# Second half of layer 0: a ring of seven gather buffers instead of four, and gathers issued six tiles ahead instead of four

## The chip, the cores and the metric

The kernel runs on one core of a Trainium2 chip. A core has five engines with a queue of instructions each: TensorE (PE, with its weight loads PEld), VectorE (DVE), ScalarE (ACT), GpSimd (POOL) and SyncE (SP). They run side by side and are tied together only by semaphores that one engine raises and another waits for. Data moves between main memory and the core's buffers by DMA, which an engine issues and which then runs by itself. The metric is the device time of one execution in microseconds (us); here the median of three runs.

## The reference, cut to what matters

The model is four graph layers over 10,000 nodes with 512 features and 10,000 edges. Layer 0 is

```python
def gnn_layer(x, W, b, src, dst):
    h = x @ W.T + b
    msgs = h[src]
    agg = jax.ops.segment_sum(msgs, dst, num_segments=N_NODES)
    return jax.nn.relu(agg)

h = gnn_layer(x, W1, b1, src, dst)
out = gnn_layer(h, W2, b2, src, dst)
...
h = jnp.maximum(_layernorm(x, axis=-1), 0.0)
x = x + _L0_gnn_ref(h, edge_index, L0_gnn_W1, L0_gnn_b1, L0_gnn_W2, L0_gnn_b2)
```

The change touches the second `gnn_layer` call (W2, b2), with the sum onto x and the layer norm's scale and bias that follow it. Rows of h are picked by source node, rows with the same destination are summed, the sums are multiplied with W2, and the result goes back to the row of its node.

## The kernel before, in words

The edges have been sorted by destination beforehand and cut into 79 tiles of 128 edges (`ET`). `layer0(..., second=True)` is the stretch from about 686 to 1058 us of the profiled execution; its buffers and semaphores carry the prefix `b_`. The sum is taken before the product, since both are linear. Per tile, all written out (no loop on the chip):

- POOL issues three indirect DMAs. `start_fetch` (L1054, the DMA in `fetch`, L815) gathers 128 rows of h into a buffer `b_G`; `residual` (also L815) gathers the rows of x that are added later into `b_xr`; `store` (`put_rows`, L819) scatters the finished rows `b_rows`. Every eighth tile POOL also computes the scales and biases of the layer norm for eight tiles (L886, L893).
- PE, in `sum_edges` (L1356), multiplies the gathered rows with a 0/1 matrix `b_sel`, which sums rows of one destination, into `b_pt` (raises `s_summed`); in `multiply` (L794 to L796) it multiplies the sums, split in a high and a low part, with W2 into `b_po` (raises `s_prod`); in `look` (L1404) it does a small look-up product for a later layer.
- DVE waits for `s_summed`, carries an open sum over from the tile before (L784, L787), takes relu(product)+x into `b_rows` (L1220, raises `s_rows`), makes the low part (L1204), the row statistics and the look-up's result (L857, L866, L1293).
- ACT waits for DVE's carry, makes the high part (L1120), six small operations that build 0/1 matrices, and last presets the product's accumulator with the bias (L1164, `b_po<-b_brow`), without which PE's next product doesn't start.

PE's order is: sum of tile u+1, product of tile u, look-up of tile u. DVE's order at step u is: carry of tile u+1, `b_rows` of tile u-1, low part of tile u+1, statistics of tile u-1. The order of POOL is given by `at(i, u, offset, ...)` in its `body`: at step u it issues the gather of tile u+4, the gather of x for tile u+2 and the store of tile u-10, in that order, so the first store comes at step 10. POOL's instructions run strictly in this order, and each wait holds up everything behind it.

Two waits on POOL matter here. The gather of tile T may overwrite its buffer only when the tile that used it four tiles ago has been summed: `wait(pool, s_summed, T.t - 3)`. With T = u+4 that is the sum of tile u. The gather of x for tile T = u+2 waits for `b_rows` of tile u-2 (`wait(pool, s_rows, T.t - 3)`).

Of the kernel before, what the change touches and what calls it, by code (L numbers as in the profile page):

```python
# [19 lines left out]
P = 128  # L20
D = 512
C = D // P
EXT = 520
# [7 lines left out]
F32, F32R, BF16 = mybir.dt.float32, mybir.dt.float32r, mybir.dt.bfloat16  # L31
# [25 lines left out]
def at(i, u, off, unroll, tiles, stage):  # L57

    tile = Tile(i + (u + off) // unroll, (u + off) % unroll, unroll)
    if not isinstance(i, int) or 0 <= tile.t < tiles:  # L60
        stage(tile)
# [17 lines left out]
def wait(eng, sem, value):  # L79

    if not isinstance(value, int) or value > 0:
        eng.wait_ge(sem, value)
# [886 lines left out]
def layer0(nc, io, g, second):  # L969
# [4 lines left out]
    NT, N, ET = g.NT, g.N, g.tiles  # L974
    U = 4
    GR = -(-ET // U)

    QUAD, RING = 8, 16 if second else 4
    LATE = 2
    if not second:  # L980
        g.hold2 = ExitStack()
        g.qrow16 = g.hold2.enter_context(nc.sbuf_tensor("qrow16", [NT, N], I16))
    qrow16 = g.qrow16
    with ExitStack() as ctx:
        e = Env(nc, ctx, "b_" if second else "a_")
# [2 lines left out]
        if second:  # L988
            s_preset = e.sem("s_preset")
        neg_half = e.sb("neghalf", [P, QUAD], F32)  # L990
        G = e.ring("G", U, [P, D if second else EXT], F32)
        sel = e.ring("sel", 2, [P, P], F32)
        carry = e.ring("carry", 2, [P, C], F32)
        Thi, Tlo = e.ring("Thi", 2, [P, C, P], F32R), e.ring("Tlo", 2, [P, C, P], F32R)
# [28 lines left out]

        s_brow, s_const = e.sem("s_brow"), e.sem("s_const")
        s_Gn = e.sem("s_Gn")
        s_G, s_x, s_put = e.sems("s_G", U), e.sems("s_x", U), e.sems("s_put", RING)
        s_sel = e.sem("s_sel")
        s_summed, s_carried, s_copied = e.sem("s_summed"), e.sem("s_carried"), e.sem("s_copied")
        s_Thi, s_Tlo = e.sem("s_Thi"), e.sem("s_Tlo")
# [21 lines left out]
        @block.gpsimd  # L1051
        def _(pool):
            def start_fetch(T):
                s = T.slot(U)  # L1054
                wait(pool, s_summed, T.t - 3)
                fetch(pool, G[s][:, :], src, index(g, "D", T, 0)).then_inc(s_G[s], 16)

            def residual(T):
                s = T.slot(U)
                wait(pool, s_rows, T.t - 3)  # L1060
                fetch(pool, xr[s][:, :], io.x, index(g, "D", T, 1)).then_inc(s_x[s], 16)

            def scales(T):
                n = ln.part(T)[1] if ln.in_last(T) else QUAD
                some = slice(T.slot(RING), T.slot(RING) + n)
                ln.make_scales(pool, T, neg_half, rows[:, some, SCALE])
                ln.make_biases(pool, T, rows[:, some, SCALE], rows[:, some, BIAS])

            def store(T):
                s = T.slot(RING)  # L1070
                if second:
                    pool.wait_ge(ln.s_bias, ln.done(T))
                else:
                    pool.wait_ge(s_rows, T.t + 1)
                put_rows(pool, g.xs[0] if second else g.h1, index(g, "D", T, 2), rows[:, s, :], N - 1)\
                    .then_inc(s_put[s], 16)

            def body(i):
                if second:
                    for u in range(RING):  # L1080
                        if u % QUAD == LATE:
                            at(i, u, -QUAD - LATE, RING, EARLY, scales)
                        at(i, u, 4, RING, ET, start_fetch)
                        at(i, u, 2, RING, ET, residual)
                        at(i, u, -QUAD - LATE, RING, EARLY, store)
                else:
                    for u in range(U):
                        at(i, u, -2, U, ET, store)
                        at(i, u, 4, U, ET, start_fetch)

            if second:
                pool.memset(one_f[:, :], 1.0)
            pool.memset(neg_half[:, :], -0.5).then_inc(s_const, 1)
            for s in range(2):
                pool.memset(carry[s][:, :], 0.0).then_inc(s_const, 1)
            if second:
                pool.memset(rows[:, :, BIAS + 1:EXT], 0.0).then_inc(s_const, 1)
            pool.wait_ge(s_const, 4 if second else 3)
            straight(-(-ET // RING), 1, 1, body, between=W and (lambda i: W.low_part(pool, i)))
            if second:  # L1100
                for first, n in LAST:
                    scales(Tile(0, first, ET))
                    for t in range(first, first + n):
                        store(Tile(0, t, ET))
            for s in range(RING):
                pool.wait_ge(s_put[s], 16 * uses(ET, RING, s))
# [239 lines left out]
        def _(pe):  # L1346
            def sum_edges(T):
                s = T.slot(2)
                pe.wait_ge(s_sel, T.t + 1)
                if second:  # L1350
                    pe.wait_ge(s_G[T.slot(U)], 16 * (T.use(U) + 1))
                else:
                    pe.wait_ge(s_Gn, T.t + 1)
                wait(pe, s_Tlo, T.t - 1)
                for c in range(C):
                    ins = pe.matmul(psum_t[s][:, c, :], G[T.slot(U)][:, c * P:(c + 1) * P], sel[s][:, :],  # L1356
                                    start=True, stop=True)
                ins.then_inc(s_summed, 1)

# [910 lines left out]
```

## Time and profile before

| | us |
|---|---|
| median of 3 runs (2797.72 to 2799.21) | 2798.69 |
| the profiled execution's own time | 2799.54 |
| its span in the profile | 2797.8 |
| PE busy in the span | 2459.9 (88%) |
| DVE, ACT, POOL busy | 2024.5 (72%), 1373.6 (49%), 1709.9 (61%) |

The profiled execution lies 0.85 us above the median; 1.7 us of it lie outside the span. Times in the rows further down are microseconds from the span's start. A row of the timeline gives start, duration, engine, line of the kernel, operation, output<-input and how many were merged; in brackets stands how long the engine was idle before it and what ended that. Matmuls are pipelined, and their ends are modelled. For a DMA that POOL issues, the row is the issue alone; the transfer itself comes later.

### The profile page before, as it was taken

Reading aid. Unit: us, or ns where it says so; the run is one execution under the profiler, and the core shown is the slowest. Engines: PE = TensorE matmul, PEld = TensorE weight load, DVE = VectorE, ACT = ScalarE, POOL = GpSimd, SP = SyncE. Lnnn points to the kernel's source line nnn. Section 1 sums busy time; section 2 is a strip of 40 time slices with the busy share of each in tenths; the row PEclk is TensorE's granted clock in tenths of the full one; section 3 lists DMA queues with packets and bytes.
Section 4 is the critical chain, followed back from the end, with each engine's and each line's share of the span. In section 5 each row is a group of like instructions: output and inputs, shape, how many; then the busy total and the mean of one; then the engine's idle time right before and its main releaser. Section 6 shows DMA issues by size and latency. Waiting matters only on the chain. (4 is left out here: it accounts for less than half of the span.)

```text
span 2797.8 us, 46999 instructions
## 1 busy us (share of the span) xinstructions
PE 2459.9 (88%) x13660; PEld 2095.8 (75%) x13660; DVE 2024.5 (72%) x5281; ACT 1373.6 (49%) x2875; POOL 1709.9 (61%) x1832
## 2 busy tenths in 40 slices
PE   3555379998988886999999969999999699999998
PEld 3344268887877776999999958888888588888886
DVE  7777666664655554888877869999999666666666
ACT  1555334454776764555555523333333245555553
POOL 0565345554566765777777647777777445555553
PEclk9999999999999998999999989999999799999999
DMA  8677643533444543343333333333334245555553
GB/s 246 206 209 206 196 125 113 146 119 114 127 134 145 156 151 127 111 129 115 113 118 114 107 110 123 114 115 114 116 120 121 85 139 153 153 153 153 153 152 110
DMA packets 145287, 385.55 MB, mean 138 GB/s; under 512 B 34127, under 2 KB 34287, under 8 KB 144554
## 3 DMA queue, kind: packets, MB, share of 16 engines
q0 software_dynamic: 100144, 300.93, 36.0%
q1 hardware_dynamic: 45002, 83.04, 9.5%
q8 instruction: 52, 0.85, 0.1%
q14 instruction: 89, 0.73, 0.1%
HBM read 259.61 MB, written 148.26 MB: 146 GB/s over the span
## 5 line engine op out<-in xcount | busy, mean ns | idle before, releaser
L1830 ACT CAST d_Thi<-d_pt 128x512 fp32r<-128x512 f32 x79 | 46.4, 587 | 307.8 <-DVE d_pt L787 276.7
L1678 PE MATMUL c_pu<-c_Zhi,parts 128*128 128x256 f32 x640 | 182.0, 284 | 5.3 <-DVE c_Zlo L1596 5.3
L1680 PE MATMUL c_pu<-c_Zhi,parts 128*128 128x256 f32 x640 | 181.8, 284 | 0.0
L1679 PE MATMUL c_pu<-c_Zlo,parts 128*128 128x256 f32 x640 | 180.6, 282 | 0.0
L815 POOL DMA_INDIRECT f_Gsrc<-rows,indexS x79 | 76.0, 962 | 170.4 <-PE f_phsrc L2159 161.4
L2075 ACT ACTIVATE f_Mhi<-f_pm 128x512 fp32r<-128x512 f32 x79 | 47.3, 598 | 262.2 <-DVE f_pm L2108 255.6
L2099 DVE TENSOR_TENSOR f_Hlosrc<-f_phsrc,f_Hhisrc 128x512 fp32r<-128x512 f32 x79 | 54.6, 692 | 159.6 <-ACT f_Hhisrc L2069 127.7
L794 PE MATMUL b_po<-parts,b_Thi 128*128 128x512 f32 x316 | 132.4, 419 | 41.0 <-issue 26.1
L819 POOL DMA_INDIRECT h<-a_rows,indexD x79 | 79.6, 1008 | 117.7 <-ACT a_rows L1172 109.0
L1565 ACT ACTIVATE c_pu<-c_pu,c_b1col 128x256 f32<-128x256 f32 x160 | 61.6, 448 | 167.6 <-PE c_pu L1680 167.6
L794 PE MATMUL d_po<-parts,d_Hhi 128*128 128x512 f32 x316 | 131.2, 415 | 1.9 <-DVE d_Hlo L1848 1.9
L794 PE MATMUL a_po<-parts,a_Thi 128*128 128x512 f32 x316 | 130.7, 414 | 0.5 <-DVE a_Tlo L1204 0.4
L794 PE MATMUL c_po<-parts,c_Uhi 128*128 128x512 f32 x316 | 127.8, 404 | 0.0
L1678 PEld LDWEIGHTS c_pu<-c_Zhi,parts 128*128 128x128 f32 x640 | 121.4, 190 | 7.6 <-DVE c_Zlo L1596 5.8
L795 PE MATMUL b_po<-parts,b_Thi 128*128 128x512 f32 x316 | 126.0, 399 | 0.0
L794 PE MATMUL f_pm<-parts,f_Hhidst 128*128 128x512 f32 x316 | 125.9, 399 | 0.0
L796 PE MATMUL f_pm<-parts,f_Hlosrc 128*128 128x512 f32 x316 | 125.9, 398 | 0.0
L796 PE MATMUL b_po<-parts,b_Tlo 128*128 128x512 f32 x316 | 125.7, 398 | 0.0
L434 POOL DMA_INDIRECT edgesD<-r_cargoD,r_posiD x79 | 75.7, 958 | 81.7 <-DVE r_posiS L399 33.2
L795 PE MATMUL f_pm<-parts,f_Hhisrc 128*128 128x512 f32 x316 | 125.5, 397 | 0.0
L795 PE MATMUL f_pm<-parts,f_Hhidst 128*128 128x512 f32 x316 | 125.2, 396 | 0.0
L794 PE MATMUL f_pm<-parts,f_Hhisrc 128*128 128x512 f32 x316 | 125.1, 396 | 0.0
(451 smaller groups left out, 9548.0 us busy)
## 6 DMA issues: line engine op xcount, KB each, us to landing
rows<-r_xt SPq DMA_DIRECT2D x40, 520.0 KB
h<-q_zerorow SPq DMA_DIRECT2D x80, 256.0 KB
r_xt<-in_x SPq DMA_DIRECT2D x80, 256.0 KB
a_wstage<-in_L_W SPq DMA_DIRECT2D x3, 1024.0 KB
selrowsD<-selD SPq DMA_DIRECT2D x1, 2640.0 KB
selrowsS<-selS SPq DMA_DIRECT2D x1, 2640.0 KB
q_keyrowD<-in_dst POOLq DMA_DIRECT2D x1, 2560.0 KB, 17.0
q_keyrowS<-in_src POOLq DMA_DIRECT2D x1, 2560.0 KB
```

What stands on the lines that cost most here:

```text
L434: pool.indirect_dma_start(g.sorted[k], bass.IndirectOffsetOnAxis(ap=posi[k][r][:, 0:1], axis=0), cargo[k][r][:, :], None).then_inc(q_moved ...
L794: ins = pe.matmul(out, hi[:, c, :], whi[:, c, :], start=start and c == 0, stop=False, skip_group_check=preset)
L795: ins = pe.matmul(out, hi[:, c, :], wlo[:, c, :], start=False, stop=False, skip_group_check=preset)
L796: ins = pe.matmul(out, lo[:, c, :], whi[:, c, :], start=False, stop=stop and c == C - 1, skip_group_check=preset)
L815: return pool.indirect_dma_start(out, None, table, bass.IndirectOffsetOnAxis(ap=rows, axis=0))
L819: return pool.indirect_dma_start(table, bass.IndirectOffsetOnAxis(ap=at_rows, axis=0), rows, None, bounds_check=last_row, oob_is_err=False)
L1565: ins = nc.scalar.activation(psum_u[:, c, :], psum_u[:, c, :], ACT.Relu, bias=b1col[:, c:c + 1])
L1678: pe.matmul(psum_u[:, o, :], g.Whi[2][:, c, cols], Zhi[:, c, :], start=c == 0, stop=False)
L1679: pe.matmul(psum_u[:, o, :], g.Whi[2][:, c, cols], Zlo[:, c, :], start=False, stop=False)
L1680: ins = pe.matmul(psum_u[:, o, :], g.Wlo[2][:, c, cols], Zhi[:, c, :], start=False, stop=c == C - 1)
L2075: nc.scalar.activation(Mhi[s][:, :], psum_m[s][:, :], ACT.Relu).then_inc(s_Mhi, 1)
L2099: dve.tensor_tensor(Hlo[k][s][:, :, :], psum_h[k][:, :, :], Hhi[k][s][:, :, :].bitcast(F32), ALU.subtract).then_inc(s_Hlo[k], 1)
```

## The change

In the second half the ring of gather buffers and their semaphores grows from 4 to 7 (`AHEAD`), the gather at step u is the one of tile u+6 instead of u+4, and it waits until the tile seven before it has been summed: with T = u+6 that is the sum of tile u-1 instead of tile u. PE reads the tile from the longer ring. The ring of x (`xr`), the stores, and the first half of the layer stay as they were.

```diff
+    AHEAD = 7 if second else 4
...
-        G = e.ring("G", U, [P, D if second else EXT], F32)
+        G = e.ring("G", AHEAD, [P, D if second else EXT], F32)
...
-        s_G, s_x, s_put = e.sems("s_G", U), e.sems("s_x", U), e.sems("s_put", RING)
+        s_G, s_x, s_put = e.sems("s_G", AHEAD), e.sems("s_x", U), e.sems("s_put", RING)
...
             def start_fetch(T):
-                s = T.slot(U)
-                wait(pool, s_summed, T.t - 3)
+                s = T.slot(AHEAD)
+                wait(pool, s_summed, T.t - AHEAD + 1)
                 fetch(pool, G[s][:, :], src, index(g, "D", T, 0)).then_inc(s_G[s], 16)
...
-                        at(i, u, 4, RING, ET, start_fetch)
+                        at(i, u, 6, RING, ET, start_fetch)
                         at(i, u, 2, RING, ET, residual)
                         at(i, u, -QUAD - LATE, RING, EARLY, store)
...
                 if second:
-                    pe.wait_ge(s_G[T.slot(U)], 16 * (T.use(U) + 1))
+                    pe.wait_ge(s_G[T.slot(AHEAD)], 16 * (T.use(AHEAD) + 1))
...
-                    ins = pe.matmul(psum_t[s][:, c, :], G[T.slot(U)][:, c * P:(c + 1) * P], sel[s][:, :],
+                    ins = pe.matmul(psum_t[s][:, c, :], G[T.slot(AHEAD)][:, c * P:(c + 1) * P], sel[s][:, :],
```

POOL's instructions at the start of the half, before the change (`b_G` gathers of h, `b_xr` gathers of x):

```order
L1097 MEMSET b_rows 128x16x6
L815 DMA b_G<-h,indexD 128x512 x3
L815 DMA b_xr<-in_x,indexD 128x512
L815 DMA b_G<-h,indexD 128x512
L815 DMA b_xr<-in_x,indexD 128x512
```

The same place with the change:

```order
L1098 MEMSET b_rows 128x16x6
L815 DMA b_G<-h,indexD 128x512 x5
L815 DMA b_xr<-in_x,indexD 128x512
L815 DMA b_G<-h,indexD 128x512
L815 DMA b_xr<-in_x,indexD 128x512
```

Two more gathers of h stand ahead of the first gather of x. From there on the two kinds alternate as before, each `b_G` now for a tile two further on. At the end of the half, POOL's instructions of before and of the change differ as follows (stores are `rows<-b_rows`):

```order
 L815 DMA b_xr<-in_x,indexD 128x512
 L819 DMA rows<-b_rows,indexD 10241x520
-L815 DMA b_G<-h,indexD 128x512
 L815 DMA b_xr<-in_x,indexD 128x512
 L819 DMA rows<-b_rows,indexD 10241x520
 L886 TENSOR_TENSOR b_rows<-b_lnvar,b_neghalf 128x8
 L893 TENSOR_TENSOR b_rows<-b_lnminus,b_rows 128x8
-L815 DMA b_G<-h,indexD 128x512
 L815 DMA b_xr<-in_x,indexD 128x512
 L819 DMA rows<-b_rows,indexD 10241x520
```

The last two gathers have moved up by two steps and are gone here. On PE, DVE and ACT the instructions and their order stay the same.

## Rows read from the trace of the kernel before

**Rows 1.** Windows: per engine busy us (count), then PE's granted clock, DMA share, GB/s.
```profile
700.00:740.00 40.00, 39.98 (x219) 33.74 (x218) 26.91 (x82) 31.82 (x79) 21.84 (x23) 1.00 0.43 123
740.00:1020.00 280.00, 246.17 (x1347) 208.12 (x1347) 163.24 (x499) 195.61 (x487) 192.47 (x198) 1.00 0.48 145
```

**Rows 2.** Waits, 686 to 1060 us: us in total, times, longest.
```profile
DVE b_carry L784 <- PE b_pt L1356: 121.0, 44, 11.3
...
POOL b_G L815 <- PE b_pt L1356: 53.2, 31, 2.6
...
PE b_pt L1356 <- DMA b_G<-h,indexD: 9.9, 1, 9.9
```

**Rows 3.** Timeline of PE before the first store: the sums of two tiles.
```profile
707.75 1.06 PE L1356 MATMUL b_pt<-b_sel,b_G 128*128 128x128 f32 x8
...
715.82 1.06 PE L1356 MATMUL b_pt<-b_sel,b_G 128*128 128x128 f32 x8
```

**Rows 4.** Timeline of DVE before the first store: the carry behind the first of them.
```profile
708.84 0.22 DVE L784 SCALAR_TENSOR_TENSOR b_carry<-b_carry,keylastD,b_pt 128x4 f32<-128x4 f32 x1 [1.28 <-PE b_pt L1356]
```

**Rows 5.** Timeline of PE in mid-half: a sum, and the next product's start.
```profile
850.41 1.06 PE L1356 MATMUL b_pt<-b_sel,b_G 128*128 128x128 f32 x8
...
856.74 0.47 PE L794 MATMUL b_po<-parts,b_Thi 128*128 128x512 f32 x1 [1.36 <-issue]
```

**Rows 6.** Timeline of DVE: a late carry, the `b_rows` behind it, the next late carry.
```profile
852.86 0.22 DVE L784 SCALAR_TENSOR_TENSOR b_carry<-b_carry,keylastD,b_pt 128x4 f32<-128x4 f32 x1 [3.28 <-PE b_pt L1356]
...
853.12 0.68 DVE L1220 SCALAR_TENSOR_TENSOR b_rows<-b_po,b_xr 128x512 f32<-128x512 f32 x1
...
862.00 0.22 DVE L784 SCALAR_TENSOR_TENSOR b_carry<-b_carry,keylastD,b_pt 128x4 f32<-128x4 f32 x1 [2.99 <-PE b_pt L1356]
```

**Rows 7.** Timeline of ACT: the preset that this product waits for.
```profile
855.92 0.67 ACT L1164 ACTIVATE b_po<-b_brow,degcol 128x512 f32<-128x512 f32 x1
```

**Rows 8.** Timeline of POOL in mid-half: issues of one double step.
```profile
853.10 0.97 POOL L815 DMA_INDIRECT b_G<-h,indexD  x1 [1.54 <-PE b_pt L1356]
854.38 0.95 POOL L815 DMA_INDIRECT b_xr<-in_x,indexD  x1 [0.30 <-issue]
855.62 1.01 POOL L819 DMA_INDIRECT rows<-b_rows,indexD  x1 [0.30 <-issue]
856.94 0.97 POOL L815 DMA_INDIRECT b_G<-h,indexD  x1 [0.30 <-issue]
858.22 0.95 POOL L815 DMA_INDIRECT b_xr<-in_x,indexD  x1 [0.30 <-issue]
859.47 1.01 POOL L819 DMA_INDIRECT rows<-b_rows,indexD  x1 [0.30 <-issue]
```

**Rows 9.** Timeline of DVE: first and last of the late carries, 32 double steps apart.
```profile
742.82 0.22 DVE L784 SCALAR_TENSOR_TENSOR b_carry<-b_carry,keylastD,b_pt 128x4 f32<-128x4 f32 x1 [2.95 <-DMA r_xt<-in_x]
...
1035.16 0.22 DVE L784 SCALAR_TENSOR_TENSOR b_carry<-b_carry,keylastD,b_pt 128x4 f32<-128x4 f32 x1 [1.97 <-PE b_pt L1356]
```

**Rows 10.** Timeline of POOL after its last gather of h: a wait for `b_rows`.
```profile
1032.93 1.02 POOL L819 DMA_INDIRECT rows<-b_rows,indexD  x1 [0.30 <-issue]
1036.38 0.98 POOL L815 DMA_INDIRECT b_xr<-in_x,indexD  x1 [2.43 <-DVE b_rows L1220]
```

**Rows 11.** Timeline of POOL in the layer's first half: a store, then a gather.
```profile
594.04 1.01 POOL L819 DMA_INDIRECT h<-a_rows,indexD  x1 [0.37 <-issue]
...
595.36 0.97 POOL L815 DMA_INDIRECT a_G<-rows,indexD  x1 [0.30 <-issue]
```

**Rows 12.** Timeline of PE and DVE there: the sum, and the carry behind it.
```profile
595.21 1.06 PE L1356 MATMUL a_pt<-a_sel,a_G 128*128 128x128 f32 x8
...
597.31 0.22 DVE L784 SCALAR_TENSOR_TENSOR a_carry<-a_carry,keylastD,a_pt 128x4 f32<-128x4 f32 x1 [1.26 <-PE a_pt L1356]
```

**Rows 13.** Timeline, first half, another place: POOL's gather and DVE's carry.
```profile
567.86 0.97 POOL L815 DMA_INDIRECT a_G<-rows,indexD  x1 [0.30 <-issue]
...
569.59 0.22 DVE L784 SCALAR_TENSOR_TENSOR a_carry<-a_carry,keylastD,a_pt 128x4 f32<-128x4 f32 x1
```

## The prediction, on record before the changed kernel ran

> **What bounds the kernel now.** I read the windows first, then the waits, then the timeline of each engine. Layer 0's second half has two regimes. Before the first store PE is busy 39.98 of 40 us; afterwards 246.17 of 280 us, at a granted clock of 1.00 in both, so about 34 us of PE's time are lost in the second regime [rows 1]. Among the waits DVE's for PE's sum is the largest (121.0 us); POOL waits 53.2 us for the same sum; PE waits for a gathered tile once in the whole half, 9.9 us at its start [rows 2]. So no gather is late after the first, and fetching earlier cannot help PE by that road.
>
> The timelines say what the second regime waits for. Early, two tiles take 715.82-707.75 = 8.07 us on PE [rows 3], and DVE's carry starts 0.03 us after the modelled end of the sum (707.75+1.06 = 708.81 against 708.84) [rows 3, 4]. In mid-half a sum ends by the model at 850.41+1.06 = 851.47, and DVE's carry, idle for 3.28 us, starts only at 852.86, 1.39 us later [rows 5, 6]; POOL, which waits for the same sum, goes on at 853.10 [rows 8]. Two engines wake together, so it is PE's signal that comes late, not DVE. From the carry on the chain is tight: ACT's preset runs 855.92 to 856.59 [rows 7], and PE's product, idle for 1.36 us, starts at 856.74 [rows 5]. Every second tile is like this: late carries stand 862.00-852.86 = 9.14 us apart [rows 6], and over 32 double steps (1035.16-742.82)/32 = 9.14 us [rows 9], against 8.07.
>
> What makes the signal late? POOL issues six transfers in a row, 0.30 us apart, then stops to wait for the sum. Its last issue before the stop is the store at 859.47, and the late carry comes at 862.00, 2.53 us behind it [rows 6, 8]. At the end of the half, where the row of issues ends with the store at 1032.93, the carry comes at 1035.16, 2.23 us behind it [rows 9, 10]. I read this as a loop: PE's signals get through about 2.2 to 2.5 us after POOL's last issue of a dense row, and POOL starts its next row only on that signal. The trace shows no cause inside the chip; the lag is what I use. One turn is carry to gather 853.10-852.86 = 0.24, gather to last store 859.47-853.10 = 6.37, store to carry 2.53; sum 9.14 [rows 6, 8].
>
> **The change, part by part.** *Seven buffers.* PE, DVE and ACT execute the same instructions; another buffer number costs nothing. *Earlier start.* Two gathers of h move ahead of the first gather of x, which is issued 2 x 1.28 us later [rows 8]. It is needed first behind the first product, and DVE's b_rows comes behind the carry anyway: I take 0; if that cover were absent, 2.6 us. The first regime stays at 8.07 us for two tiles, since POOL there has two transfers per tile only.
>
> *The moved wait.* At step u the gather now needs the sum of tile u-1, which is long done when POOL gets there. POOL doesn't stop there any more, but one instruction later, at the gather of x, which waits for b_rows of tile u-2. DVE makes those rows behind the late carry: carry 852.86, b_rows 853.12+0.68 = 853.80 [rows 6]. Queued behind this wait are the store, the next gather and the rest of the row. So the row of six is now x, store, gather, x, store, gather, and it ends with a gather. Its turn of the loop:
> - carry to x: the one place that shows it has the carry at 1035.16 and the x gather, released by b_rows, at 1036.38: 1.22 us [rows 9, 10] (instead of 0.24).
> - x to last gather: x to store 1.24, to gather 1.32, to x 1.28, to store 1.25, to gather 1.32 as the one before: 6.41 us [rows 8] (instead of 6.37).
> - last gather to carry: not shown in this half, where every such row ends with a store. In the layer's first half a store at 594.04 is followed by a gather at 595.36; the sum ends by the model at 595.21+1.06 = 596.27 and the carry comes at 597.31, 1.95 us behind the gather [rows 11, 12]. At another place the gather is at 567.86 and the carry at 569.59: 1.73 us [rows 13]. I take their mean, 1.84 (instead of 2.53 after a store).
>
> Sum 1.22+6.41+1.84 = 9.47 us, +0.33 per double step. Bounds: if the signals get through 2.53 us behind the last store however a gather follows, the turn is 1.22+5.09+2.53 = 8.84 (x to last store 859.47-854.38 = 5.09), -0.30; if a gather holds them as long as a store, 1.22+6.41+2.53 = 10.16, +1.02. I take the middle value, since in rows 11 and 12 the store lies 597.31-594.04 = 3.27 us back when the carry comes, so the gather did hold it.
>
> *The steps with the norm's scales*, one in four, put two computations behind a store; I give them the same +0.33. *The end.* The last two gathers are gone there, some 2.6 us of POOL's time; the last of its waits is for b_rows and not for them [rows 10]. I take 0, bounded by the 2.43 us of that wait.
>
> Sum: 32 x 0.33 = +10.6 us. From the profiled execution's 2799.54 that is 2810.1; it lies 0.85 above the median of 2798.69, so the forecast is 2809.
>
> Two statements of the Trainium skill speak against the loop. The rows show signals late by 1.39 us beside POOL's issues [rows 5, 6]. "Trainium Architecture — The Big Picture", section "What this means for kernel authors", says that the sides of SBUF for engines and for DMA can't contend; by it the loop would not run over POOL's transfers, and the time would stay as it is. "Perfetto Trace Analysis", section "Summary: the profiler window per engine type", says that a matmul's end is only an estimate, so the lag could lie in the matmul itself; the trace disagrees in so far as the same sum of 1.06 us was followed at once, in 0.03 us, before the stores began [rows 3, 4].
>
> **The rivals.**
> 1. *The trailing gather holds nothing.* PE's signals wait for the last store only: 32 x -0.30 = -9.6 us, 2789. For it: in this half the lag was only seen behind stores, and early, where POOL issues gathers alone, it is 0.03. Against it: rows 11 to 13.
> 2. *The moved wait is free.* The lag has another cause that keeps its rhythm, for instance PE's own, and POOL's wait is slack. Then 2798.7. For it: the skill's rule above, and that PE never waits for POOL by name [rows 2].
> 3. *The lag goes away.* With its tie to the sum gone, POOL's row falls otherwise against PE's signals and they pass. Then two tiles take 8.07 as in the first regime: 32 x (8.07-9.14) = -34 us, 2764. POOL could nearly follow: six issues take 6.37+1.3 = 7.7 us. Against it: POOL still stops once per double step on something that hangs on PE's late signal.
> 4. *A gather holds as long as a store*: 32 x 1.02 = +33 us, 2831. Here the place is the same as in the forecast, the price the upper bound.
> The other side of the forecast is rival 1: it decides from the point where the signal gets through less than 9.14-1.22-6.41 = 1.51 us behind the gather.
>
> **How the numbers follow.** Forecast 0.46 (own range 2803 to 2818), rival 1 0.22, rival 2 0.12, rival 3 0.12, rival 4 0.08. The range leaves out rival 3 and most of rival 4: 2785 to 2824. A measurement of this kernel tells 0.2%, 5.6 us, from no change. Faster: rivals 1 and 3, less a little of 1 that falls within 0.2%: 0.32. Same: rival 2 and the edges of the forecast and of rival 1: 0.19. Slower: 0.49.
>
> **What would show it.** In the profile of the changed kernel: POOL's waits for PE at b_G gone, and in their place waits at b_xr for DVE's b_rows, some 30 of 1.5 to 3 us; the last issue before each a b_G; late carries about 9.5 us apart and 1.7 to 2.0 us behind that b_G; PE's busy share between 740 and 1020 us a little lower; the first regime, at 8.07 for two tiles, and the other layers unchanged. Carries 8.8 us apart are rival 1, 8.1 rival 3. It would be wrong if POOL's waits stay at b_G, or if the distance of the carries doesn't follow POOL's last issue.

## The result, and the profile after

| | before | after |
|---|---|---|
| median, us | 2798.95 (4 runs) | 2831.81 (4 runs, 2829.46 to 2834.04) |
| after / before | | 1.0116, 95% interval 1.0099 to 1.0134 |
| profiled execution, its span | 2799.54, 2797.8 | 2829.46, 2827.7 |

The change costs 33 us, 1.2%. The forecast was 2809 with a range of 2785 to 2824, so the direction was right, and the time lay outside the range, 1 us above rival 4 (2831). All comparisons here and below are of executions in the fast state; one of the six of e13_pad, 5040 us long, was not and is left out. Lines behind the new one carry a number higher by 1 than before: `b_pt` is summed in L1357, `b_rows` made in L1221.

The windows of the changed kernel (same stretches as [rows 1]; columns as there):

```profile
700.00:740.00 40.00, 36.54 (x194) 30.65 (x193) 22.22 (x69) 26.33 (x65) 18.38 (x20) 0.96 0.42 125
740.00:1020.00 280.00, 243.31 (x1238) 204.10 (x1237) 150.41 (x464) 181.73 (x451) 178.65 (x184) 0.93 0.43 131
```

Both stretches changed. In the second PE ran 1238 instructions where it ran 1347, at nearly the same busy time (243.31 against 246.17 us), with a granted clock of 0.93 instead of 1.00. In the first, before any store, 3.4 us of PE are gone, which the prediction had at nothing. The waits between 686 and 1092 us (total us, times, longest) say who now waits for whom:

```profile
DVE b_carry L784 <- PE b_pt L1357: 90.0, 42, 11.3
POOL b_xr L815 <- DVE b_rows L1221: 85.5, 39, 4.7
...
PE b_pt L1357 <- DMA b_G<-h,indexD: 9.9, 1, 9.9
```

POOL's 53.2 us at `b_G` [rows 2] have become 85.5 us at `b_xr`, and PE waits once for a gather, 9.9 us, as before. The timeline of POOL in mid-half shows the row of six that ends with a gather, and the stop behind it:

```profile
860.10 0.96 POOL L815 DMA_INDIRECT b_xr<-in_x,indexD  x1 [0.30 <-DVE b_rows L1221]
861.37 1.01 POOL L819 DMA_INDIRECT rows<-b_rows,indexD  x1 [0.30 <-issue]
862.68 0.98 POOL L815 DMA_INDIRECT b_G<-h,indexD  x1 [0.30 <-issue]
864.01 0.95 POOL L815 DMA_INDIRECT b_xr<-in_x,indexD  x1 [0.35 <-DVE b_rows L1221]
865.26 1.02 POOL L819 DMA_INDIRECT rows<-b_rows,indexD  x1 [0.30 <-issue]
866.59 0.98 POOL L815 DMA_INDIRECT b_G<-h,indexD  x1 [0.30 <-issue]
870.19 0.94 POOL L815 DMA_INDIRECT b_xr<-in_x,indexD  x1 [2.63 <-DVE b_rows L1221]
```

DVE's carries around it, one per double step (they answer to [rows 6]):

```profile
839.27 0.22 DVE L784 SCALAR_TENSOR_TENSOR b_carry<-b_carry,keylastD,b_pt 128x4 f32<-128x4 f32 x1 [3.68 <-PE b_pt L1357]
...
849.26 0.22 DVE L784 SCALAR_TENSOR_TENSOR b_carry<-b_carry,keylastD,b_pt 128x4 f32<-128x4 f32 x1 [3.66 <-DMA r_xt<-in_x]
...
858.88 0.22 DVE L784 SCALAR_TENSOR_TENSOR b_carry<-b_carry,keylastD,b_pt 128x4 f32<-128x4 f32 x1 [3.25 <-PE b_pt L1357]
...
868.98 0.22 DVE L784 SCALAR_TENSOR_TENSOR b_carry<-b_carry,keylastD,b_pt 128x4 f32<-128x4 f32 x1 [3.32 <-DMA r_xt<-in_x]
...
878.84 0.22 DVE L784 SCALAR_TENSOR_TENSOR b_carry<-b_carry,keylastD,b_pt 128x4 f32<-128x4 f32 x1 [3.73 <-PE b_pt L1357]
```

From 839.27 to 878.84 are four turns of 9.89 us on average. The parts of a turn are: carry 868.98 to x gather 870.19 is 1.21, x to last gather as in the row above it 866.59-860.10 = 6.49, last gather 866.59 to carry 868.98 is 2.39. (Two of the rows name a DMA of another layer as the releaser. The carry waits for PE's sum there too; the profile infers releasers.)

Not every turn has this form. In 24 of the 32 double steps between tiles 12 and 76 POOL stops behind a gather and the carry comes 1.96 to 2.46 us behind it (once 3.21). In the other eight POOL computes the norm's scales just then, and the carry follows its sum by 0.03 to 0.52 us; the one at 858.88 is of these.

Nor is every signal held that PE raises while POOL issues. In the kernel before, between tiles 12 and 76 and away from the scales, 16 sums ended behind the third issue of a row, and their carries came 0.03 to 0.21 us behind them; 16 ended behind the sixth, and theirs came 0.91 to 1.11 us behind. The first kind, in the row that starts at 862.23 (before; POOL's third issue is at 864.76):

```profile
863.75 1.06 PE L1356 MATMUL b_pt<-b_sel,b_G 128*128 128x128 f32 x8
...
864.84 0.22 DVE L784 SCALAR_TENSOR_TENSOR b_carry<-b_carry,keylastD,b_pt 128x4 f32<-128x4 f32 x1
```

So "held until the row ends" describes the signals raised late in a row, or just behind it, and not those of its first three issues.

PE's products in two places, the first behind an idle time of 2.96 us (compare [rows 5], where the same instruction takes 0.47):

```profile
754.21 0.72 PE L794 MATMUL b_po<-parts,b_Thi 128*128 128x512 f32 x1 [2.96 <-ACT b_po L1165]
754.72 0.63 PE L795 MATMUL b_po<-parts,b_Thi 128*128 128x512 f32 x1
...
1071.13 0.47 PE L794 MATMUL b_po<-parts,b_Thi 128*128 128x512 f32 x1
```

These two are the products of tiles 12 and 76. They lie 316.92 us apart; before it was 1039.05-746.70 = 292.35. That is 9.90 us per double step against 9.14, +24.6 us over 32. Behind 12 of 16 idle times of 1.9 to 3.1 us PE ran at the lower of its clock's two levels (1.2 GHz; granted 0.50 from 755 to 757 us, and from 953 to 959 us) for 3 to 6 us; the 12 products there take 4.3 to 5.5 us where the other 52 take 3.03.

The rest is the start. POOL and DVE there:

```profile
699.43 0.95 POOL L815 DMA_INDIRECT b_G<-h,indexD  x1 [0.30 <-issue]
700.68 0.95 POOL L815 DMA_INDIRECT b_xr<-in_x,indexD  x1 [0.30 <-issue]
701.93 0.95 POOL L815 DMA_INDIRECT b_G<-h,indexD  x1 [0.30 <-issue]
```

```profile
705.41 0.22 DVE L784 SCALAR_TENSOR_TENSOR b_carry<-b_carry,keylastD,b_pt 128x4 f32<-128x4 f32 x1 [8.60 <-DMA r_xt<-in_x]
```

POOL issues 13 gathers without a stop, the last at 701.93. The sum of tile 2 ends by the model at 701.66, and its carry comes at 705.41, 3.5 us behind the last gather. Before, the row had ten gathers, the last at 697.41, and that carry came 0.04 us behind its sum, at 700.76. The product of tile 12 comes 67.36 us after the first gather instead of 60.61: 6.75 us. Of these 5.4 us are there at tile 4 (32.05 instead of 26.63 us) and 1.3 with tile 12 itself, the first whose signal is late in mid-half. The sum is 24.6 + 6.75 = 31.3, which is what the half has grown by from its first gather to its last product (368.15 to 399.50).

### The profile page after: what moved, and what is told of

It is laid out like the page before. It is cut to its first block and busy times, and to the rows that moved or that the text cites. A ratio compares the mean times of both kernels' runs of the same rounds, so it can differ in the third digit from the quotient of the medians.

```text
span 2827.7 us, 46999 instructions
## 1 busy us (share of the span) xinstructions
PE 2481.2 (88%) x13660; PEld 2113.1 (75%) x13660; DVE 2024.2 (72%) x5281; ACT 1375.7 (49%) x2875; POOL 1712.3 (61%) x1832
## 5 line engine op out<-in xcount | busy, mean ns | idle before, releaser
L794 PE MATMUL b_po<-parts,b_Thi 128*128 128x512 f32 x316 | 141.0, 446 | 50.8 <-ACT b_po L1165 49.2
L815 POOL DMA_INDIRECT b_xr<-in_x,indexD x79 | 75.1, 951 | 101.0 <-DVE b_rows L1221 85.5
L784 DVE SCALAR_TENSOR_TENSOR b_carry<-b_carry,keylastD,b_pt 128x4 f32<-128x4 f32 x79 | 17.1, 217 | 165.5 <-PE b_pt L1357 90.0
L795 PE MATMUL b_po<-parts,b_Thi 128*128 128x512 f32 x316 | 133.7, 423 | 0.0
L796 PE MATMUL b_po<-parts,b_Tlo 128*128 128x512 f32 x316 | 133.6, 423 | 0.0
L794 PE MATMUL f_pm<-parts,f_Hhidst 128*128 128x512 f32 x316 | 126.0, 399 | 0.0
L795 PE MATMUL f_pm<-parts,f_Hhisrc 128*128 128x512 f32 x316 | 125.3, 396 | 0.0
```

What stands on the lines that cost most here:

```text
L794: ins = pe.matmul(out, hi[:, c, :], whi[:, c, :], start=start and c == 0, stop=False, skip_group_check=preset)
L795: ins = pe.matmul(out, hi[:, c, :], wlo[:, c, :], start=False, stop=False, skip_group_check=preset)
L796: ins = pe.matmul(out, lo[:, c, :], whi[:, c, :], start=False, stop=stop and c == C - 1, skip_group_check=preset)
L815: return pool.indirect_dma_start(out, None, table, bass.IndirectOffsetOnAxis(ap=rows, axis=0))
```

## The experiments

Theory A is the prediction's loop, with a gather that holds PE's signals as long as a store: PE's signals get through some 2.3 us behind POOL's last issue of a dense row, and POOL starts the next row only on what hangs on them. Kernels that ran together share the runs of the kernel before; a ratio is to these. The expected times in the quoted expectations are on one scale, on which the kernel before takes 2795 to 2799 us. "Hold" is the distance from POOL's last DMA issue to a late carry (one more than 0.2 us behind its sum), "restart" that from the carry to POOL's next DMA issue, both as means over some 30 such carries, worked out from the timelines. For the kernel before they are 2.44 and 0.35 us, for the change 2.31 and 1.18; "turn" is two tiles' share of the distance between the products of tiles 12 and 76.

**The strict wait again (e1_strict).**

```diff
-                wait(pool, s_summed, T.t - AHEAD + 1)
+                wait(pool, s_summed, T.t - (5 if second else 3))
```

> Seven buffers and gathers six tiles ahead, but the gather at step u waits for the sum of tile u again, as before the change. Theory A (POOL's moved wait makes the longer rows of issues, and PE's signals get through some 2.4 us behind the last issue of such a row): in the middle of the half POOL pauses where it did before, a double step takes 9.14 us again and PE's granted clock between 740 and 1020 us is 1.00; only the longer row of 13 gathers at the start stays, some 6 us: 2805 (2801 to 2809). Rival B (what costs is that seven tiles are kept and in flight, whatever POOL waits for): 2830, as the change.

Measured 2799.03 against 2795.03: 1.0012 (1.0003 to 1.0022), so 3.4 us remain of 33; on a before of 2799 that is 2802, in theory A's range. The window of the middle:

```profile
740.00:1020.00 280.00, 247.84 (x1354) 209.39 (x1353) 163.75 (x502) 197.41 (x490) 194.44 (x199) 1.00 0.49 146
```

1354 instructions of PE and a clock of 1.00 are those of before [rows 1]. POOL waits at `b_G` for the sum again (45.7 us), hold 2.30, restart 0.36, turn 9.06. The product of tile 4 is 4.0 us late by the start. So the ring of seven and the distance of six cost nothing in the middle; the moved wait costs it all. And the hold is that of the change: between the two kernels the turn differs by the restart, 0.82 us x 32 = 26 us, measured 316.92-289.91 = 27.0.

**The loose wait, four ahead (e2_four).**

```diff
-                wait(pool, s_summed, T.t - AHEAD + 1)
+                wait(pool, s_summed, T.t - (4 if second else 3))
...
-                        at(i, u, 6, RING, ET, start_fetch)
+                        at(i, u, 4, RING, ET, start_fetch)
```

> Seven buffers, but gathers four tiles ahead as before, and the wait loosened as in the change (the gather at step u waits for the sum of tile u-1). Theory A: the row of ten gathers at the start is that of before, so the first four tiles cost nothing more, and the middle goes as in the change, with POOL stopping at b_xr and the clock at 0.93: 2831 less 6 = 2825 (2820 to 2829). Rival B (the distance of six tiles is what costs): 2799, as before.

It took 2818.79 us, 1.0088 (1.0064 to 1.0112). On a before of 2799 that is +24.6 us, where theory A had 26 and rival B none. Hold 2.19, restart 1.18, turn 9.70. The first row has 11 gathers and not the ten of before, since the loosened wait lets one more through, and the product of tile 4 is 1 us late.

**A shorter row at the start (e3_start).**

```diff
-                wait(pool, s_summed, T.t - AHEAD + 1)
+                wait(pool, s_summed, T.t - (AHEAD - 1 if T.t > 6 else 3))
```

> The change, but the gathers of tiles 4, 5 and 6 wait for the sums of tiles 0, 1 and 2, three or four tiles back, so that the half doesn't begin with 13 gathers in one row. Theory A (a row of gathers alone holds PE's signals if it is long enough): carry of tile 2 within 0.1 us of its sum instead of 3.75, product of tile 4 some 6 us earlier; middle as in the change: 2825 (2821 to 2829). Rival (the start's 6 us have another cause, such as more gathers in flight): 2831.

It took 2826.47 us, 1.0115 (1.0095 to 1.0135): nothing gained, and on a before of 2799 that is 2831, the rival's number. The carry of tile 2 is prompt, as expected, but the gather of tile 4, released by the first sum at 690.14, starts a row that goes on, with one stop of 2.7 us, to 707.57. Now the sum of tile 4 is held, and its carry comes at 710.36, 5.0 us late:

```profile
701.23 0.22 DVE L784 SCALAR_TENSOR_TENSOR b_carry<-b_carry,keylastD,b_pt 128x4 f32<-128x4 f32 x1 [1.06 <-PE b_pt L1357]
710.36 0.22 DVE L784 SCALAR_TENSOR_TENSOR b_carry<-b_carry,keylastD,b_pt 128x4 f32<-128x4 f32 x1 [6.24 <-PE b_pt L1357]
```

The expectation was wrong in that a wait in front does not make the row shorter, it moves it. That gathers of h and x, without a store, can be followed by a held signal is read off this timeline; the run's time doesn't tell it from the rival, more gathers in flight.

**A stricter wait (e4_every).**

```diff
-                wait(pool, s_summed, T.t - 3)
+                wait(pool, s_summed, T.t - (2 if second else 3))
```

> The kernel before with four buffers, but the gather at step u waits for the sum of tile u+1 instead of tile u, so that POOL has to pause at each tile, after three issues and not six. Theory A1 (only a row of about five or more issues holds PE's signals): signals pass, two tiles take 8.07 us as before the first store: 2765 (2760 to 2780). Theory A2 (the end of any row holds them for 2.4 us): a turn per tile of 3 x 1.28 + 2.4 + 0.24 = 6.4 us instead of 4.57, 66 times: 2920 (2880 to 2940). Rival C (PE's signals are late for a reason of PE's own): 2799 to 2805.

The ratio is 1.0002 (0.9992 to 1.0011), neither A1 nor A2, and the number is that of rival C (a reason of PE's own). POOL still issues six in a row: two sums lie 3.9 us apart on PE and three issues take 3.84, so the second sum is there when POOL comes to ask. Only the late carries changed from even to odd tiles, as POOL's stop did. So they go by POOL's rows, and a rhythm of PE's own, which the edit left alone, doesn't explain them. The run does not tell A1 from A2.

**PE kept busy (e5_warm).** Ahead of the product of each fourth tile (core of the edit):

```diff
+                if T.t >= 12 and T.t % 4 == 0:
+                    for c in range(6):
+                        pe.matmul(psum_f[:, :], g.Whi[slot][:, 0, 0:P], g.Whi[slot][:, 1, :], start=True, stop=True)
```

> The change, and PE runs six products of weights with weights (128x512, some 0.23 us apart, into a bank that nobody reads) ahead of the product of each fourth tile from 12 on, in the place where PE stood idle for 1.9 to 3 us in the change. They are 17 x 1.4 = 24 us of extra PE work. Theory A (PE's idle stretches of 2 to 3 us let the granted clock fall, and the product behind them takes 4.4 to 4.6 us instead of 3.03): the slow products go, the clock between 740 and 1020 us rises from 0.93 to 0.98 or more, POOL's waits stay; the time falls by up to 18 us, 2813 (2808 to 2825) on the scale on which the change took 2831. Rival B (the clock's fall costs nothing, since PE waits anyway): 2831. Rival C (the extra products push the loop out by their own time): 2831 to 2855.

It took 2830.21 against 2800.74 us: 1.0100 (1.0083 to 1.0117); the change had 1.0116 (1.0099 to 1.0134).

```profile
740.00:1020.00 280.00, 252.64 (x1326) 211.15 (x1325) 151.46 (x469) 183.29 (x454) 179.29 (x184) 0.98 0.43 132
```

The clock is back at 0.98, 4 slow products are left of 12, and the turn is 9.85 instead of 9.90. The interval, 2822 to 2832 on a before of 2799, reaches a little into theory A's range; the turn decides for rival B: with two thirds of the slow products gone it is 0.05 us shorter, 1.7 us over the half. The fall of the clock follows from PE's waiting and has at most a small price of its own, as I read it because a product that ends earlier finds the signals still held. It isn't nothing: the carry of tile 54 in the change came 3.21 us behind POOL's last issue, 0.04 us behind its sum, and PE was late there with a product of 5.46 us.

**Three buffers of sums and products (e6_three, e7_three).** Core of the edit, on the kernel before and on the change:

```diff
-        psum_t = [e.ps(f"pt{i}", [P, C, P]) for i in range(2)]
-        psum_o = [e.ps(f"po{i}", [P, D]) for i in range(2)]
+        psum_t = [e.ps(f"pt{i}", [P, C, P]) for i in range(SUMS)]
+        psum_o = [e.ps(f"po{i}", [P, D]) for i in range(SUMS)]
...
-                    at(i, u, 1, U, ET, sum_edges)
+                    at(i, u, SUMS - 1, U, ET, sum_edges)
```

> The kernel before (four gather buffers), with three instead of two of each of psum_t, Thi and psum_o in this half, and PE sums two tiles ahead of its product instead of one. A late signal of a sum then has 3.9 us to arrive before anything waits on it. Theory A with free POOL: PE never waits for a signal, a tile takes 4.04 us instead of 4.57: 64 x 0.53 = 34 us less, 2761 where before takes 2795. Theory A with POOL's loop (POOL still has to stop, and signals come only 2.4 us behind its last issue, but its row grows to nine issues, three tiles): (9 x 1.28 + 1.5)/3 = 4.34 us per tile, 15 us less: 2780 (2770 to 2788). Rival (the time is set by something other than the late signals): 2795.

> The same three buffers of sums and products, put on the change, with six gather buffers instead of seven and gathers five tiles ahead (the memory holds no more); the gather at step u waits for the sum of tile u-1, as in the change. Theory A: the moved wait cost time only through PE's late signals; with these covered it costs nothing or gains, so this takes the time of the three buffers on the kernel before or less (2755 to 2785). Rival B (longer rows of POOL's issues are bad by themselves): some 25 us above that run.

e6_three took 1.0030 (1.0019 to 1.0042), e7_three 1.0043 (1.0028 to 1.0057). Before the first store a tile takes 3.91 us instead of 4.04, and then the gain is lost. POOL can now go on for longer, and it does, here for twelve issues and the scales without a stop, from 839.94 to 855.99:

```profile
842.47 1.02 POOL L819 DMA_INDIRECT rows<-b_rows,indexD  x1 [0.30 <-issue]
843.49 1.71 POOL L886 TENSOR_TENSOR b_rows<-b_lnvar,b_neghalf 128x8 f32<-128x8 f32 x1
...
855.99 1.01 POOL L819 DMA_INDIRECT rows<-b_rows,indexD  x1 [0.30 <-issue]
858.94 0.97 POOL L815 DMA_INDIRECT b_G<-h,indexD  x1 [1.94 <-DMA r_xt<-in_x]
```

```profile
850.60 1.06 PE L1357 MATMUL b_pt<-b_sel,b_G 128*128 128x128 f32 x8
```

```profile
858.70 0.22 DVE L784 SCALAR_TENSOR_TENSOR b_carry<-b_carry,keylastD,b_pt 128x4 f32<-128x4 f32 x1 [2.63 <-DMA r_xt<-in_x]
```

The sum of that carry ended at 851.66, 7 us before; DVE itself was ready for it only at 856.07, so 2.63 us of the 7 are DVE's wait, and before that it had waited 3.72 us for a product. The carry is 2.71 us behind POOL's last issue. Both forms of theory A missed, and the rival (no change) is the nearest: the room that PE gained is eaten by POOL's longer rows. The moved wait itself costs little here (1.0043 against 1.0030, intervals overlap; 64 tiles take 305.0 against 299.2 us in the two profiles).

**POOL thinned out (e8_thin, e11_thin4).** The gathers of x are taken from POOL, on the change and on the kernel before; SP loads other rows of x instead:

```diff
+            if second:
+                for t in range(ET):
+                    wait(sp, s_rows, t - 3)
+                    sp.dma_start(xr[t % U][:, :], io.x[bass.ds(min(t * P, NODES - P), P), :]).then_inc(s_x[t % U], 16)
...
-                        at(i, u, 2, RING, ET, residual)
```

> The change, but POOL doesn't gather x: SP loads 128 consecutive rows of x per tile with a plain DMA instead, so the rows that are added are not those of the tile's nodes. POOL has two issues per tile, 2.56 of 4.0 us. Theory A (a dense row of POOL's issues holds PE's signals): in the middle carries follow their sums within 0.1 us, no slow product, clock 1.00, a tile takes 4.04 us as before the first store: from 4.95, 64 x 0.91 = 58 us less, 2770 (2760 to 2780). Rival B (the scatters, or the traffic of the transfers themselves, hold them): lags of 1 us and more stay, 2800 or more.

> The kernel before (four buffers, gathers four ahead, strict wait), but POOL doesn't gather x: SP loads 128 consecutive rows of x per tile, so the rows that are added are not those of the tile's nodes. With the same edit the change took 0.9945 of before. Theory A (the change costs only through POOL's dense rows): with POOL thin the moved wait costs nothing; this takes the same time as that run, or 1 to 6 us less by the start: 0.993 of before (0.990 to 0.996). Rival B (longer ring and earlier gathers cost in themselves): 0.984 or less, that is still some 25 us less than that run.

e8_thin took 0.9945 (0.9928 to 0.9962), e11_thin4 0.9905 (0.9888 to 0.9921). The first is 2784 on a before of 2799, above theory A's range of 2760 to 2780; the second lies in its range. With the strict wait (e11_thin4) PE goes through the middle with hardly a stop:

```profile
740.00:1020.00 280.00, 274.13 (x1483) 233.37 (x1482) 182.67 (x560) 219.00 (x540) 154.21 (x156) 0.99 0.54 162
```

Its timeline has POOL mostly in rows of two with 1.7 us between them (117.0 us of waits at `b_G` for the sum), and no late signal up to tile 75; a tile takes 264.15/64 = 4.13 us. DMA is busier there than in any other run, 0.54 of the time, so the amount of traffic as such holds nothing. At the end of the half, where the gathers are over, the same kernel issues a gather and eight stores in one row, from 993.74 to 1004.15, and the sum of tile 76, ended at 1000.81, is seen at 1006.60: 5.79 us late, 2.45 us behind the last store:

```profile
1004.15 0.98 POOL L819 DMA_INDIRECT rows<-b_rows,indexD  x1 [0.30 <-issue]
...
1006.60 0.22 DVE L784 SCALAR_TENSOR_TENSOR b_carry<-b_carry,keylastD,b_pt 128x4 f32<-128x4 f32 x1 [6.96 <-DMA r_xt<-in_x]
```

With the loose wait (e8_thin) most tiles are prompt as well, but once in eight tiles POOL, let go behind the scales, issues six in a row, and then a signal is late again:

```profile
841.22 1.02 POOL L815 DMA_INDIRECT b_G<-h,indexD  x1 [0.16 <-POOL b_rows L893]
842.55 1.03 POOL L819 DMA_INDIRECT rows<-b_rows,indexD  x1 [0.30 <-issue]
843.88 0.99 POOL L815 DMA_INDIRECT b_G<-h,indexD  x1 [0.30 <-issue]
845.17 1.01 POOL L819 DMA_INDIRECT rows<-b_rows,indexD  x1 [0.31 <-issue]
846.49 0.98 POOL L815 DMA_INDIRECT b_G<-h,indexD  x1 [0.30 <-issue]
847.77 1.02 POOL L819 DMA_INDIRECT rows<-b_rows,indexD  x1 [0.31 <-issue]
```

```profile
850.02 0.22 DVE L784 SCALAR_TENSOR_TENSOR b_carry<-b_carry,keylastD,b_pt 128x4 f32<-128x4 f32 x1 [2.90 <-DMA r_xt<-in_x]
```

850.02 is 2.25 us behind the last issue, and 1.64 behind the sum's end. So theory A's core holds (signals come late behind dense rows, and in time with thin ones), and its expectation that the moved wait would be free here was wrong: it costs 0.4% (277.02 against 264.15 us for 64 tiles, 12.9 us), as I read it since the strict wait had been what kept POOL's rows short. The two runs don't tell whether POOL's issuing or the transfers of its indirect DMAs do the holding, since the edit takes away both.

**What ends the row (e9_xgs, e10_gsx).** On the change, order x, gather, store; on the kernel before, gather, store, x:

```diff
-                        at(i, u, 6, RING, ET, start_fetch)
                         at(i, u, 2, RING, ET, residual)
+                        at(i, u, 6, RING, ET, start_fetch)
```

> The change, with POOL's order within a step turned from gather, x, store to x, gather, store. POOL still stops at b_xr for b_rows, but its row of six now ends with a store and not with a gather of h. Theory A (a gather that ends a row holds PE's signals as long as a store does, 2.2 to 2.5 us): the turn stays at 1.22 + 6.4 + 2.3 to 2.5 = 9.9 to 10.1 us per double step, time as the change, 1.012 times before (1.009 to 1.014). Rival B (the last issue's kind matters, a gather holds less, as the prediction had it with 1.84): the turn would now be 10.2, and the time some 10 us above the change.

> The kernel before with POOL's order within a step turned from gather, x, store to gather, store, x. POOL stops at b_G for the sum as before, and its row of six ends with the gather of x. Theory A (any kind of issue holds the signals equally from its start): the turn stays at 0.24 + 6.4 + 2.2 to 2.5, time within 0.3% of before. Rival B (a store holds longest since its transfer is a scatter of finished rows; a row that ends with x lets PE's signals through 0.2 to 0.7 us earlier): 32 x 0.2 to 0.7 = 6 to 22 us faster than before.

e9_xgs took 1.0102 (1.0085 to 1.0119), hold 2.19 behind a store; e10_gsx 1.0010 (1.0000 to 1.0019), hold 2.26 behind a gather of x. Both times lie in theory A's ranges; the turn of e9_xgs, 9.71, is a little under its 9.9 to 10.1, and far from rival B's 10.2. The kind of the last issue moves the hold by 0.2 us at most.

**Six buffers of x (e12_x6, e15_x6).** e12_x6 is e6_three with this edit; e15_x6 has it with the loose wait, five gather buffers and gathers four ahead:

```diff
-                s = T.slot(U)
-                wait(pool, s_rows, T.t - 3)
+                s = T.slot(XR)
+                wait(pool, s_rows, T.t - XR + 1)
```

> Three buffers each of psum_t, Thi and psum_o, sums two tiles ahead of the product, as in the run that took 1.003 of before, and besides six buffers of x instead of four, so that the gather of x at step u waits for b_rows of tile u-4 instead of u-2. There POOL's rows were broken by a wait for b_rows after four issues. Theory A (one stop of POOL costs about 1.5 us beside its issues, and what counts is how many tiles go between two stops): rows of nine issues, (9 x 1.28 + 1.5)/3 + 0.23 for the scales = 4.57 us per tile, as before or a little less: 0.997 to 1.001. Rival B (longer rows only hold PE's signals longer, and PE runs out of buffers meanwhile): 1.003 or more.

> The change's moved wait with less memory: five gather buffers, gathers four tiles ahead, the gather at step u waits for the sum of tile u-1; besides six buffers of x instead of four, so that the gather of x at step u waits for b_rows of tile u-4 and POOL no longer stops there. Theory A (the moved wait costs since POOL restarts at b_xr 1.2 us behind the late carry instead of 0.3 us at b_G): POOL stops at b_G again, restarts 0.3 us behind the carry, the turn is 0.3 + 6.4 + 2.4 = 9.1 us: 1.000 of before (0.998 to 1.003). Rival B (a looser wait lets POOL's rows grow, and that is what costs): 1.008 to 1.012, with rows of nine and more issues.

e12_x6 took 1.0051 (1.0034 to 1.0068), rival B. e15_x6 took 1.0161 (1.0144 to 1.0178), the slowest of all: theory A's expectation of 1.000 fell, and rival B had the mechanism and too low a price (1.008 to 1.012). The restart is 0.23 us, as it had said. But POOL, which both waits now let go further, issues nine in a row, ending here:

```profile
864.88 0.95 POOL L815 DMA_INDIRECT b_xr<-in_x,indexD  x1 [0.30 <-issue]
866.13 1.01 POOL L819 DMA_INDIRECT rows<-b_rows,indexD  x1 [0.31 <-issue]
868.94 0.97 POOL L815 DMA_INDIRECT b_G<-h,indexD  x1 [1.80 <-PE b_pt L1358]
```

```profile
862.56 1.06 PE L1358 MATMUL b_pt<-b_sel,b_G 128*128 128x128 f32 x8
```

```profile
868.71 0.22 DVE L784 SCALAR_TENSOR_TENSOR b_carry<-b_carry,keylastD,b_pt 128x4 f32<-128x4 f32 x1 [6.34 <-PE b_pt L1358]
```

The sum ends at 863.62 and is seen at 868.71, 5.1 us late and 2.58 us behind the last issue. PE, with two buffers of sums, stands still meanwhile; eight tiles take 326.90/8 = 40.9 us. So the loop's price has a second factor beside the restart, the length of the row, and in the change it was the wait at `b_xr` that still kept the row at six.

**Wider spacing (e13_pad, e14_half).** A scratch tile is cleared behind each store, of 512 or 256 columns:

```diff
+                if second:
+                    wait(pool, s_pad, T.t)
+                    pool.memset(pad[:, 0:512], 0.0).then_inc(s_pad, 1)
```

> The kernel before, and POOL clears a scratch tile of 128x512 (some 0.5 us) behind each store, so that three issues take 4.34 us and not 3.84. Theory A1 (what holds PE's signals is that POOL issues faster than something drains, and a little more distance per tile empties it): signals pass, POOL is the bound at 4.3 to 4.4 us per tile instead of 4.57: 0.995 of before (0.993 to 0.997). Theory A2 (the signals come 2.2 to 2.4 us behind the last issue before a real stop, however the row is spaced): the turn grows by the one or two clearings in it, 9.14 + 0.5 to 1.0: 1.006 to 1.011.

> The same with a scratch tile of 128x256 (some 0.3 us). Theory A1: 4.1 to 4.2 us per tile if this distance is enough: 0.991; if not, as before or slower. Theory A2: turn 9.14 + 0.3 to 0.6: 1.003 to 1.007.

They took 1.0039 (1.0025 to 1.0053) and 1.0033 (1.0019 to 1.0047). The first fits neither form; the second lies in A2's range. In e13_pad the late carries no longer keep a rhythm: some pairs of tiles pass at once, others wait 3.8 us. Spreading the same issues to 4.28 us per tile doesn't free the signals. What ends the hold inside the chip stays open.

No version that computes the reference was faster than the kernel before; the two that were (e8_thin, e11_thin4) add other rows of x.

## Why the prediction was wrong

**The loop: right in the main.** POOL's waits moved from `b_G` to `b_xr`, 39 of them, its last issue before the long ones is a gather, and in 23 of 24 double steps the late carry follows that issue by 1.96 to 2.46 us. e1_strict shows that the place of the wait is the cause, e8_thin and e11_thin4 that POOL's dense rows are. What the loop left out is that the length of the row isn't given but set by the waits: e6_three, e12_x6 and e15_x6 missed by it.

**Carry to x, 1.22: right** (1.18). This term alone makes the middle slower: e1_strict to the change, 27.0 us.

**x to last gather, 6.41: right** (6.43 from 840.48 to 846.91, 6.49 in the row shown).

**Last gather to carry, 1.84: the step that failed.** It is 2.31. The value was the mean of two places in the layer's first half [rows 11 to 13], where POOL issues two transfers per tile and its rows are short. One of the two measures no hold at all. The sum of [rows 13] ended only at 568.11+1.06 = 569.17, and DVE was at work until 569.56, 0.03 us before the carry at 569.59:

```profile
568.11 1.06 PE L1356 MATMUL a_pt<-a_sel,a_G 128*128 128x128 f32 x8
...
568.80 0.76 DVE L1211 SCALAR_TENSOR_TENSOR a_po<-a_brow,degcol,a_po 128x512 f32<-128x512 f32 x1 [1.66 <-PE a_po L796]
```

The 2.23 us of [rows 9, 10], which the loop was also read from, are of the same kind: the sum ended at 1035.08 and the carry came 0.08 us behind it. A distance from POOL's last issue says something only where the sum had ended well before the carry, as in [rows 5, 6]. The bound of 2.53 from the half itself [rows 6, 8] was the nearer row in the length of the row, too, and I set it aside because it ended with a store. e9_xgs and e10_gsx show that the end's kind hardly matters. 32 x (2.31-1.84) = 15 us.

**Earlier start, 0: failed.** It is 6.75 us. I had asked only whether x came in time, not what three more issues do to a row. The carry of tile 2 came 0.04 us behind its sum with ten gathers in the first row (before), 0.91 us with 11 (e2_four), 3.99 us with 12 (e1_strict) and 3.75 us with 13 (the change), and 3.1 to 3.5 us behind the row's last issue in the three that were late; in e3_start a row of nine gathers is followed by a carry 5.0 us late. That the row is the cause, and not the number of gathers in flight, is argued from these timelines; no run's time decides it. That the first regime stays at 8.07 us per two tiles was right from tile 4 on.

**End, 0: right.** From the start of tile 76's product to the end of tile 78's it is 15.22 us against 15.19. **Scales, the same as elsewhere: not quite.** The 16 double steps around the scales (of tiles 16 to 20, 24 to 28 and so on, by the carries) grew by 0.52 us each, from 9.20 to 9.72, the 16 others by 1.01, from 9.07 to 10.09.

The sum with the measured terms: 32 x (1.18 + 6.41 + 2.31 - 9.14) = 24.3, and 6.75 for the start, 31.1 of the 31.3 measured in the half. That it comes out so closely is partly luck, since eight of the 32 double steps don't have this form. Rival 4 named the mechanism, with a chance of 0.08. That its 2831 lies within 1 us of the result is luck, too: it had 33 us in the middle, where 24.6 were measured, and nothing for the start.

**Not foreseen:** the granted clock, 0.93 in the middle. It looks like a cost (64 products take 212.8 us instead of 194.3), and e5_warm shows that most of it isn't one.

**The two statements of the Trainium skill.** Signals of PE that come late beside POOL's issues were in every run with dense rows (1.39 us in [rows 5, 6], 1.64 to 5.1 us in the rows above), and in e11_thin4 only behind its one dense row. "Trainium Architecture — The Big Picture", section "What this means for kernel authors", says that the engines' and the DMA's sides of SBUF can't contend; by the prediction's reading of it the time would have stayed, and it moved by 33 us. That doesn't contradict the sentence itself, which is on these sides alone; where the signals are held instead, no run here shows. "Perfetto Trace Analysis", section "Summary: the profiler window per engine type", has a matmul's end as an estimate; a sum that is seen 1.39 us behind its modelled end in the kernel before [rows 5, 6] and 0.04 us behind it with POOL thinned out (e11_thin4) has its lag from POOL, not from the estimate.

## What to carry to other kernels

A wait that looks idle may be what paces a queue: before loosening one, ask how many issues the engine will then send in one row, and what is held until the row ends. When a missing duration is bounded by two rows, take the one from the same density of work, not the one with the same kind of instruction, and look first whether the engine that wakes was waiting at all. And when a slower clock appears beside a longer wait, find out first which one came of the other.

## What was not expected of the hardware

Where PE's sums ended late in a row of six to nine indirect DMAs that POOL issued 0.3 us apart, or just behind it, the semaphore signals arrived some 2.0 to 2.6 us behind the last of them, whatever their kind (2.39 in the change, 2.45 in e11_thin4, 2.58 in e15_x6), and 3.5 us behind the last of 13 in the change. Signals raised behind the third issue of such a row arrived in 0.03 to 0.21 us (kernel before). They were prompt too (0.04 us) with rows of two issues and 1.7 us between them, at a higher share of DMA time (e11_thin4, 0.54 against 0.43 in the change). In the change PE's granted clock was at the lower level (0.50) for 3 to 6 us behind 12 of its 16 idle times of 1.9 to 3.1 us in mid-half, and a product took 4.3 to 5.5 us instead of 3.03.
